# Weight preparation beside the first chunk, five reordered plans and single-pass bias rows in a two-layer recurrent kernel

## What is computed

```python
# first layer, recurrent branch
xz = x_norm @ in_proj_w;  xi, z = split(xz)
xc = silu(causal_conv4(xi) + conv_b)
dt, Bm, Cm = split(xc @ x_proj_w);  dt = softplus(dt @ dt_proj_w + dt_proj_b)
h  = exp(dt * -exp(A_log)) * h + dt * Bm * xc      # 16 states a channel, 512 channels
y  = sum(h * Cm, -1);  y = (y + D * xc) * silu(z);  out = y @ out_proj_w
# gated branch, blocks of 16
scale = max(max|v| / 6, 1e-12);  q = round_to_grid(v / scale) * scale
# second layer weights
w = (qweights / 7.5 - 1) * scales + lora_b @ lora_a
```

## Time and profile before

| | us |
|---|---|
| median of three runs | 1848.96 (1847.87 to 1852.0) |
| the profiled execution | 1856.52 |
| its span on the core | 1854.7 |
| PE, DVE busy | 1577.4 (85%), 1551.4 (84%) |
| ACT, POOL busy | 1437.5 (78%), 1252.4 (68%) |

### The profile page before, as it was taken

How to read it: one execution, slowest core, us unless ns; L and a number is a source line. 1 busy time by engine, 2 the same in 40 slices (tenths; PEclk the granted TensorE clock), 3 DMA queues, 4 the chain that set the end, 5 groups by cost and what they waited for, 6 DMA issues and landing times.

```text
span 1854.7 us, 28175 instructions
## 1 busy us (share of the span) xinstructions
PE 1577.4 (85%) x7632; PEld 1164.4 (63%) x7632; DVE 1551.4 (84%) x2882; ACT 1437.5 (78%) x3076; POOL 1252.4 (68%) x1313
## 2 busy tenths in 40 slices
...
DMA packets 68395, 91.70 MB, mean 49 GB/s; under 512 B 15674, under 2 KB 34686, under 8 KB 68238
## 3 DMA queue, kind: packets, MB, share of 16 engines
...
## 4 chain that ended last, share of the span: by engine, by line
PE 27%; POOL 20%; DVE 16%; issue 16%; ACT 12%; POOLq 0%; ACTq 0%; DVEq 0%; DMA 0%
PE bank L511 10%; POOL drive L965 10%; PE bank L627 6%; DVE unit L1127 4%; DVE hc L1133 3%; PE bank L516 2%; PE y_ps L537 2%; ACT unit L742 2%; PE bank L498 1%; PE bank L563 1%; ACT op_a L709 1%; DVE xc L1158 1%; ACT L709 1%; ACT L923 1%; POOL s L1068 1%
## 5 line engine op out<-in xcount | busy, mean ns | idle before, releaser
L965 POOL TENSOR_TENSOR drive<-wx,rows 128x1024 f32<-128x1024 f32 x256 | 604.1, 2360 | 163.3 <-DVE unit L1127 82.8
L1127 DVE TENSOR_TENSOR_SCAN unit<-unit,drive 128x512 f32<-128x512 f32 x512 | 616.7, 1221 | 30.7 <-POOL drive L971 23.4
L742 ACT ACTIVATE unit<-dt,aneg 128x254 f32<-128x254 f32 x1024 | 441.9, 468 | 19.8 <-ACT carry L750 0.7
L1133 DVE TENSOR_TENSOR hc<-unit,rows 128x512 f32<-128x512 f32 x512 | 340.9, 684 | 8.8 <-issue 3.0
L537 PE MATMUL y_ps<-ident,hc 128*128 128x128 f32 x2048 | 278.1, 282 | 52.5 <-DVE hc L1133 52.4
L537 PEld LDWEIGHTS y_ps<-ident,hc 128*128 128x128 f32 x2048 | 241.2, 145 | 115.3 <-DVE hc L1133 71.8
L742 ACT ACT_TABLE_LOAD x109 | 139.8, 1283 | 3.7
L750 ACT ACTIVATE carry<-unit 128x4 f32<-128x4 f32 x512 | 79.3, 169 | 66.8 <-DVE unit L1140 63.0
L627 PE MATMUL bank<-op_a,w_f 128*128 128x256 f32 x512 | 115.7, 385 | 11.2 <-ACT op_a L709 11.2
L709 ACT ACT_TABLE_LOAD x77 | 98.8, 1283 | 22.4 <-PE bank L498 21.6
L511 PE MATMUL bank<-w_f,wide 128*128 128x256 f32 x512 | 113.3, 379 | 1.5 <-ACT wide L709 1.5
(11 more groups left out here) (220 smaller groups left out, 3439.4 us busy)
## 6 DMA issues: line engine op xcount, KB each, us to landing
rows<-rows_scratch SPq DMA_DIRECT2D x256, 256.0 KB, 3.3
x_t<-in_L_attn_x_dram SPq DMA_DIRECT2D x16, 256.0 KB, 3.7
x<-in_L_attn_x_dram SPq DMA_DIRECT2D x16, 256.0 KB, 3.3
out_dram<-x SPq DMA_DIRECT2D x16, 256.0 KB, 2.1
...
```

Of the source, the lines that this page charges most:

```text
L742: last = a_.activation(u[:, k * TOK:(k + 1) * TOK].rearrange("p (b t) -> p b t", b=B)[:, :, 1:TC], dt[p][:, g, :].rearrange("p (b t) -> p ...
L965: g_.tensor_tensor(drive[n % 2][:, :, :].rearrange("p (g b) t -> p g b t", b=B), wx[p][:, :, :].rearrange("p g (b t) -> p g b t", b=B), ro ...
L1127: v.tensor_tensor_scan(u[:, :], u[:, :], d, 0.0, ALU.mult, ALU.add).then_inc(S["scan_done"], 1)
L1133: v.tensor_tensor(hc[n % NPROD][:, 4 * half:4 * half + 4, :].rearrange("p (g b) t -> p g b t", b=B), unit_of(ch, n, half)[:, :].rearrange( ...
```

## The change

It has four parts.

1. The block for the weights and the loop's block become one. The loads are grouped into four semaphores, and the input of the first chunk is loaded first. The steps of the first chunk that lead up to its scans (`FRONT`) stand ahead of the loop, between the steps of the weight preparation. Weights not yet turned lie in buffers of the loop. The turns and folds write to the two `y_ps` banks instead of three. Every engine waits for the last of the 38 turns and folds before it enters its plan.
2. A bias row is no longer an fp32 matmul of 6 rows: the rows are split into a high and a low part of type F32R in 64 rows (`b_two`), picked by `pick`, in one matmul.
3. Waits that another wait implies are left out, in `exp`, `out`, `drive`, `scan` and `hc`.
4. All five plans are written in another order.

```diff
+FRONT = {
+    "SP": ("load", "wr"),
+    "POOL": ("f", "log"),
+    "ACT": ("xn", "xhf", "u", "tap0", "tap1", "z0", "tap2", "tap3", "z1", "xc0", "xc1", "usave", "xp", "dt0", "dt1",
+            "dtexp", "dtln"),
+    "PE": ("uT", "xi0", "xi1", "z0", "xi2", "xi3", "z1", "xp", "dt0", "dt1"),
+    "DVE": ("f", "conv0", "conv1", "dt", "wx"),
+}
...
-                return t.matmul(dst[:, 0:wide_ * D], ident[0:NROW, row:row + 1].to_broadcast([NROW, P]),
-                                b_rows[:, None, :].to_broadcast([NROW, wide_, D]), start=False, stop=True,
+                return t.matmul(dst[:, 0:wide_ * D], pick[:, row:row + 1].to_broadcast([2 * LOW, P]),
+                                b_two[:, None, :].to_broadcast([2 * LOW, wide_, D]), start=False, stop=True,
...
-                act.wait_ge(*at("dt_ready", ch))
+                if (n, half) == (0, 0):
+                    act.wait_ge(*at("dt_ready", ch))
...
-                dve.wait_ge(*at("drive_ready", ch, 2 * n + 2))
+                if half == 0:
+                    dve.wait_ge(*at("drive_ready", ch, 2 * n + 2))
...
-                dve.wait_ge(*rows_in(ch, n))
...
              @block.sync
             def _(sp):
...
+                    sp_step(sp, "load", 0)
+                    for dst, src in load_front:
+                        sp.dma_start(dst, src).then_inc(front_in, 16)
+                    for dst, src in load_lora:
+                        sp.dma_start(dst, src).then_inc(lora_in, 16)
+                    for dst, src in load_gate:
+                        sp.dma_start(dst, src).then_inc(gate_in, 16)
+                    for dst, src in load_rest:
+                        sp.dma_start(dst, src).then_inc(rest_in, 16)
+                sp_step(sp, "wr", 0)
+                sp.wait_ge(turn_out, N_TURNS)
...
              @block.gpsimd
             def _(pool):
...
+                pool_step(pool, "f", 0)
+                divide(0)
+                divide(1)
+                unscale(0)
+                divide(2)
+                pool_step(pool, "log", 0)
+                unscale(1)
+                unscale(2)
+                pool.wait_ge(rest_in, 16 * len(load_rest))
+                pool.wait_ge(turn_out, N_TURNS)
...
              @block.tensor
             def _(pe):
...
+                pe.wait_ge(rest_in, 16 * len(load_rest))
+                for n, (dst, parts) in enumerate(rest_turns):
+                    turn_in(parts, N_LB + N_FOLD + n)
+                pe.wait_ge(w_out_done, 3)
+                for n, (dst, parts) in enumerate(gate_turns):
+                    turn_in(parts, N_LB + N_FOLD + N_REST + n)
...
              @block.vector
             def _(dve):
...
+                dve_step(dve, "f", 0)
+                dve.wait_ge(lora_in, 16 * len(load_lora))
+                v.tensor_scalar(l_raw, q_raw, 1.0 / 7.5, -1.0, ALU.mult, ALU.add).then_inc(lora_deq, 1)
+                dve_step(dve, "conv0", 0)
...
+                dve_step(dve, "conv1", 0)
+                dve.wait_ge(gate_in, 16 * len(load_gate))
+                scale(0)
+                scale(1)
+                round_(0)
+                scale(2)
+                round_(1)
+                dve_step(dve, "dt", 0)
+                dve_step(dve, "wx", 0)
+                round_(2)
...
 DVE_PLAN = """
-    clr15a- xround yg- scan0a clr15b- hc0a scan0b clr0a hc0b clr0b scan1a hc1a clr1a scan1b scan2a hc1b clr1b
+    hc15b- wx clr15a- yg- scan0a clr15b- hc0a scan0b clr0a hc0b clr0b scan1a scan1b hc1a clr1a hc1b op- clr1b
...
```

More of the change, by code:

```diff
@@ L37 @@
 XW = NTAP - 1 + TC
+LOW = 32
 MAGIC = 1.5 * 2 ** 22
@@ L79 @@
+    h2T-- g11 u01 sum1 sum2 u2T- u10 u11 f10- sum3 sum4 f11- f12- f13- sum5 b2a-- uT+ f2- b2T-- xi0+ xi1+ sum6
+    z0+ xn1T- xi2+ xi3+ sum7
 """
 ACT_PLAN = """
[L81 to L84 removed]
@@ L88 @@
+    exp1a s1-- out0a yg0- usave out0b yg1- exp1b exp2a out1a exp2b g00 out1b g01 out2a opn- g10 h2-- g11 exp3a
+    out2b exp3b exp4a out3a u2- exp4b out3b xn+ exp5a out4a xhf+ exp5b out4b exp6a f10- f11- f12- out5a out5b
+    f13- exp6b exp7a out6a u+ out6b exp7b out7a b2n-- exp8a exp8b b2g-- tap0+ tap1+ hn- z0+ out7b xn1- tap2+
+    tap3+ xc0+ out8a z1+ xc1+ exp9a exp9b out8b exp10a out9a xp+
 """
 POOL_PLAN = """
-    drive14- drive15- b1-- arg fix0 drive0 xout fin--- drive1 drive2 hb1-- drive3 fix1 f+ drive4 op- drive5 j0in
@@ L91 @@
-    hb2-- drive6 s0b- drive7 b2-- drive8 j0out j1in x1- drive9 drive10 diff- j1out b0- hb0- drive11 xin+ drive12
-    drive13 log+
+    drive14- drive15- b1-- arg xout fix0 drive0 fin--- drive1 hb1-- drive2 drive3 op- drive4 f+ drive5 fix1
+    drive6 s0b- drive7 j0in drive8 hb2-- b2-- j0out j1in x1- drive9 hb0- diff- drive10 j1out b0- xin+ drive11
+    drive12 drive13 log+
 """
 DVE_PLAN = """
-    clr15a- xround yg- scan0a clr15b- hc0a scan0b clr0a hc0b clr0b scan1a hc1a clr1a scan1b scan2a hc1b clr1b
@@ L96 @@
-    hc2a scan2b clr2a hc2b op- clr2b scan3a scan3b h2-- hc3a hc3b clr3a clr3b ug0 scan4a scale0 ug1 hc4a scan4b
-    clr4a hc4b scan5a clr4b scan5b hc5a xscale+ hc5b clr5a clr5b round0 scan6a b2s-- hc6a scale1 scan6b clr6a
-    hc6b scan7a hc7a clr6b scan7b clr7a hc7b clr7b x1- scan8a conv0+ scan8b hc8a hc8b clr8a conv1+ round1 b0s-
-    clr8b scan9a scan9b hc9a hc9b clr9a clr9b scan10a hc10a scan10b clr10a scan11a score- scan11b hc10b hc11a
-    clr10b hc11b clr11a attn- clr11b h1- scan12a hc12a scan12b hc12b clr12a clr12b scan13a hc13a clr13a f++
@@ L101 @@
-    scan13b b1s- hc13b clr13b scan14a scan14b hc14a hc14b clr14a clr14b dt+ scan15a wx+ scan15b hc15a hc15b
+    hc15b- wx clr15a- yg- scan0a clr15b- hc0a scan0b clr0a hc0b clr0b scan1a scan1b hc1a clr1a hc1b op- clr1b
+    scan2a hc2a h2-- clr2a scan2b hc2b clr2b ug0 scan3a hc3a scan3b clr3a hc3b clr3b scan4a hc4a scale0 clr4a
+    scan4b scan5a hc4b ug1 clr4b xscale+ scan5b scan6a hc5a clr5a hc5b hc6a clr5b clr6a round0 scan6b hc6b
+    scan7a clr6b b2s-- scan7b hc7a clr7a scale1 hc7b x1- conv0+ scan8a clr7b scan8b hc8a hc8b clr8a clr8b conv1+
```

469 lines of the change are left out of this document (246 added, 223 removed).

## The result

The changed kernel takes 2014.51 us (2013.01 to 2016.13, 4 runs) against 1849.46 (1847.87 to 1852.0): ratio 1.0891, 95% interval 1.0872 to 1.091. It is 165 us slower. The profiled execution took 2016.13 us, its span was 2014.3.

What follows compares the result with a forecast made beforehand. DVE was taken as the bound, every new wait adding to it. First scan 100, scans 1769.3 and drain 98 made 1967.3, with 1.8 more 1969.1, times 0.996 about 1960 us; own range 1925 to 1995, wide 1850 to 2020.

Steps and rivals of the forecast that it cites:

- rival C: Loop: PE's clock falls to 0.88, giving 1985 us, or 2020 with more late work; 0.17 beyond 1995, shared with another rival.
- the sign of below 0.95: Loop: PE's granted clock below 0.95 was named as something that would show the forecast right.
- the two waits on PE's chains: DVE's waits per period for products of `ug0`, 2.55 us, and for statistics at `b1s`, 2.35 us; both 0 before.
- First scan, 100: Front: loads and weight preparation end sooner, first scan at 97 to 104.5 us, taken 100, against 184.5.
- The case with contention: Weight preparation: DVE and POOL hold each other up, adding some 7.5 us, all turned at 92.5 instead of 85.
- The list of stalls: Loop: fourteen places in the new order where DVE waits on a chain, summing to 16.15 us a period.
- `conv0`: DVE stall of 1.65 us a period: `b2` behind `drive8` and `hb2` on POOL, then ACT steps ahead of `tap0`.
- The period, 112.85: Loop: 96.1 us without stalls, plus 16.15 of stalls and 0.6 of clears and `hc`; 13.1 more than before.
- Bias rows and drain: Single-pass rows save 0.8 us each: PE 94 to 89 us a period, drain 101.4 to 98, -3.5.
- The factor 0.996: Whole time: the earlier median 1848.96 over its profiled execution 1856.52, scaling 1969.1 to 1961 us.
- A: Loop: stalls run beside each other, DVE bound by its own work; 1761 us, or 1720 with period 97; chance 0.12.
- B: Loop: about half of the 13.1 us a period arrives, 1859 us; chance 0.14.

Runs made afterwards that it cites:

- mix_poolsp_new: front_oldplans with POOL's and SP's plans of the changed kernel, the other plans staying old: 1988.84 us, ratio 1.0751 to the kernel before.
- front_oldplans: The changed kernel with the five plans of the kernel before: 1767.09 us, ratio 0.9543 to the kernel before.
- front_fp32bias: front_oldplans with the two-pass fp32 bias rows of before: 1781.58 us, ratio 0.9625 to the kernel before.
- after_swaps: The changed kernel with two swaps in PE's plan, b1a ahead of sum12 and u00 beside u01 behind g11: 1987.96 us, ratio 1.0746.
- wx: The changed kernel with the DVE step wx moved back ahead of scan15b: 2028.19 us, ratio 1.0947 to the kernel before.
- fin: front_oldplans with fin behind drive1 on POOL instead of ahead of it: 1812.43 us, ratio 0.9788 to the kernel before.
- mix_pool_old: The changed kernel with POOL's old plan: 2149.98 us, ratio 1.1622 to the kernel before.

## Why the prediction was right, point by point

**Direction and cause.** Right: slower, by the orders, with DVE's waits as the place. The forecast was 1960 and the time is 2014.5, so the loss against before was 111 forecast and 165 measured. That lies above the forecast's own range (1925 to 1995) and inside the wide one only near its top, which was there for rival C. The granted clock of 0.96 in the loop is not rival C's 0.88, and the sign of below 0.95 did not come either; the two waits on PE's chains were 2.7 and 2.4 where 2.55 and 2.35 stood. So it was luck that a margin kept for a slow PE covered what was short elsewhere: from 1969.1 to the 2016.1 of the profiled execution the first scan adds 8.9, fifteen periods 33.6, the term of 4 for the first chunk 5.7 (it is 9.7), and the drain takes 1.1 off.

**First scan, 100.** 108.9. The gate group landed at 36.8, not 30.5, and the doubling beside POOL was real: L1366 took 4.6 us where it takes 1.2 alone, `dt` 4.6 for 1.2, the two scales 1.6 and 2.3 for 0.22. Turned at 98.4 against 92.5 with contention. The 14 turns took 9.2, not 14. The case with contention is what happened, and the first scan is 4.4 us beyond its end of 104.5. On this point the rule of the Trainium skill (SBUF — State Buffer, section "SBUF: two separate sides") fits the trace: `dt` started at 75.64, beside POOL's product from 75.5 to 79.2, and ended 1.1 us after it, and the first L1366, from 46.86 to 51.45, ended 1.1 us after the divide that had begun at 45.77 and ended at 50.36. So the later one waited for the earlier one to end, as that section says, and did not share with it. The products that the prediction set against this (`hc`, 0.69 us) often lay beside POOL and took 0.69 all the same; they read a unit, in PSUM. The products of 704 elements with both inputs in SBUF (L943, L945), 0.89 us each, lay beside no POOL instruction in the four periods, so they test nothing.

**The list of stalls.** Sum 16.15 forecast, 16.3 measured (all waits over 0.15 us). Over four periods, in us a period (forecast in brackets): `ug0` 2.7 (2.55), `b1s` 2.4 (2.35), `scan0a` 1.47 (1.5), `scan1a` 1.26 (1.3), `scan3a` 1.05 (1.05), `round0` 1.0 (0.95), `scan12a` 0.84 (0.9), `op` 0.8 (0.8), `scan10b` 0.71 (0.85), `attn` 0.7 (0.6), `scan14b` 0.49 (0.65), `scan11a` 0.41 (0.5), `scan15a` 0.37 (0.5), `conv0` 0.4 (1.65), and one that I did not list, `score` 1.8. The earlier trace rows have 0.7 a period for it before the change, and the sum put it at nothing. The two misses, -1.3 and +1.8, nearly cancel, which is luck. The chain booked for `conv0` shows in mix_poolsp_new, at `scan7b`.

**The period, 112.85.** 115.07. The idle time agrees: (460.26 - 385.55) / 4 = 18.7 against 16.15 + 2.2 + 0.6 = 18.95. The step that was mis-sized is the busy time of DVE: I kept 93.95 and it is 96.4. Two small instructions make most of it. `j_scl` and `x_scl` lie beside the POOL products of `j0out` and `s0b`, and take 1.33 and 0.85 us a period, where front_oldplans has 0.42 for the two `j_scl` together and 0.18 for `x_scl`: 1.6. The rounding of 512 elements (L941) takes 0.70 instead of 0.43, and 0.1 is on the product `xs` (L1041). The instructions' own times add up to 1.84 a period more than before; the remaining 0.6 is that neighbours on DVE overlap less, which may be the 0.6 that I had booked as idle time for clears and `hc` side by side, but no run shows that. The 2.45 are 37 us in all, two thirds of the miss.

**Bias rows and drain.** -3.5 forecast for the drain, -4.5 measured, of which front_fp32bias gives 2.1 to the bias rows (102.4 against 100.3). PE's busy time fell by 3.5 a period in front_oldplans against front_fp32bias, not by 5.

**The factor 0.996.** The profiled execution of the changed kernel took 2016.13 with a median of 2014.51, so scaling by the ratio of before took 8 us off that should have stayed. Two slips did not move the forecast: nine of the fourteen stalls are under 1.1 us, not ten, and the period below which it is faster is 99.7 + 5.9 = 105.6, not 105.4.

**The rivals.** A and B said that stalls run beside each other. As a statement on the order as written they were wrong: it came nearly whole. As one on what an edit brings they were right: both swaps took 2.4 of 5.1 us off the period, `wx` made it 1.3 longer instead of 1.2 shorter, and `fin` 3.5 longer instead of 1.2 shorter.

What stays open: how much of the 15 us that POOL's and SP's new orders cost the old ones is SP's, why `ug0` and `yg` wait so long in mix_pool_old, and how much of after_swaps' missing gain is the clock of 0.92 and how much PE's later sums.
